# Token mixing, attention and FFN on one Trainium2 core: SyncE issues the loads of the next x behind the first sequence's probability exchange

## The reference

```
h = tok(x)                               # (64, 128, 192): per block of 16 rows q, k, v by small
                                         # matrices over the rows, softmax(q k'), q + attn v
h = h + attention(layernorm(h))          # 12 heads of 64, 3 kv heads, rope, softmax, Wo
h = h + ffn(layernorm(h))                # gelu(h @ W_in.T + b) @ W_out, 192 -> 768 -> 192
```

## Time and profile before

| | |
|---|---|
| median of 3 runs | 1170.94 us (1169.92 to 1171.51) |
| the profiled execution | 1165.9 us |
| its span, first to last instruction | 1163.6 us |
| PE busy | 995.3 us (86%) |
| DVE busy | 804.1 us (69%) |
| GpSimd (POOL) busy | 680.6 us (58%) |
| ACT busy | 664.2 us (57%) |
| SyncE's DMA queue | 121.05 MB, 37.9% of the 16 DMA engines' span |
| mean granted TensorE clock | 0.938 |

### The profile page before, as it was taken

How to read it: one execution, slowest core, us unless ns; L and a number is a source line. 1 busy time by engine, 2 the same in 40 slices (tenths; PEclk the granted TensorE clock), 3 DMA queues, 4 the chain that set the end, 5 groups by cost and what they waited for, 6 DMA issues and landing times.

```text
span 1163.6 us, 25886 instructions
## 1 busy us (share of the span) xinstructions
PE 995.3 (86%) x7402; PEld 836.9 (72%) x7402; DVE 804.1 (69%) x1996; ACT 664.2 (57%) x2501; POOL 680.6 (58%) x968
## 2 busy tenths in 40 slices
PE   7778988889888889888898888898888988888988
PEld 4667867768677677677686776776776867767777
DVE  4777766677667686666777676766767776767673
ACT  2555665646556556556565565655555655646564
POOL 2667565466655575655666555655556665556672
PEclk9999989899899899898999898998999998989999
DMA  5153334433344333344333443334443334433341
GB/s 169 28 136 108 92 104 133 124 99 88 88 133 133 98 102 87 112 133 119 98 93 88 133 133 97 100 85 117 133 119 108 85 88 133 133 97 94 102 116 48
DMA packets 193423, 124.68 MB, mean 107 GB/s; under 512 B 30720, under 2 KB 184960, under 8 KB 193408
## 3 DMA queue, kind: packets, MB, share of 16 engines
q1 hardware_dynamic: 190528, 121.05, 37.9%
q10 hardware_dynamic: 2880, 3.44, 0.9%
HBM read 69.39 MB, written 55.05 MB: 107 GB/s over the span
## 4 chain that ended last, share of the span: by engine, by line
PE 57%; DMA 16%; DVE 11%; SPq 9%; issue 5%; POOL 1%; ACT 1%; DVEq 0%; POOLq 0%
PE ring L1088 12%; PE ring L952 11%; PE ring L881 9%; DMA spill<-EB 8%; DMA ET<-spill 8%; PE bank L900 7%; PE ring L919 4%; DVE rot_s L597 4%; PE ring L859 3%; SPq L254 3%; SPq L236 3%; PE ring L1020 2%; PE bank L1055 2%; SPq L235 2%; PE ring L1047 2%
## 5 line engine op out<-in xcount | busy, mean ns | idle before, releaser
L330 ACT ACTIVATE E<-ring,m_neg 128x128 f32<-128x128 f32 x768 | 271.6, 373 | 17.0 <-DVE m_neg L603 16.0
L488 POOL TENSOR_TENSOR E<-E,e_rcp 128x512 f32<-128x512 f32 x158 | 176.6, 1126 | 40.4 <-DVE e_rcp L626 37.6
L480 POOL TENSOR_TENSOR qkT<-rot_c,rot_s 128x256 f32<-128x256 f32 x256 | 187.8, 734 | 20.1
L952 PE MATMUL ring<-ET,v_tok 128*64 128x512 f32 (+1 forms) x256 | 83.6, 799 | 111.9 <-DMA ET<-spill 111.5
L330 ACT ACTIVATION_READ_ACCUMULATOR E<-ring,m_neg 128x1 f32 x768 | 161.5, 210 | 0.0
L478 POOL TENSOR_TENSOR rot_s<-rot_s,rope_qs 128x256 f32<-128x256 f32 x192 | 145.9, 760 | 9.6 <-DVE rot_s L597 9.6
L1088 PE MATMUL ring<-wo_sb,OT 128*128 128x192 f32 x744 | 147.3, 352 | 0.0
L603 DVE TENSOR_REDUCE m_neg<-ring 128x4 f32<-128x512 f32 x192 | 129.9, 678 | 21.0 <-PE ring L919 21.0
L465 POOL TENSOR_SCALAR ve<-mv 128x1 f32<-128x1 f32 x64 | 14.0, 219 | 222.5 <-DVE mv L574 219.3
L900 PE MATMUL bank<-wout_sb,G 128*128 128x192 f32 x744 | 144.0, 330 | 0.0
L1088 PEld LDWEIGHTS ring<-wo_sb,OT 128*128 128x128 f32 x744 | 135.4, 211 | 8.7 <-issue 8.7
(11 more groups left out here) (156 smaller groups left out, 2646.3 us busy)
## 6 DMA issues: line engine op xcount, KB each, us to landing
spill<-EB SPq DMA_DIRECT2D x186, 256.0 KB, 2.7
ET<-spill SPq DMA_DIRECT2D x248, 128.0 KB, 2.8
ET<-spill SPq DMA_DIRECT2D x248, 64.0 KB, 2.4
x_sb<-in_x_dram SPq DMA_DIRECT2D x64, 192.0 KB, 2.5
out_dram<-out_sb SPq DMA_DIRECT2D x31, 192.0 KB, 2.1
x_sb<-in_x_dram SPq DMA_DIRECT2D x64, 64.0 KB, 2.3
w_raw<-in_w_att_dram ACTq DMA_DIRECT2D x2, 608.0 KB, 4.9
win_raw<-in_w_in_dram ACTq DMA_DIRECT2D x2, 384.0 KB, 6.1
```

The source lines that it names most:

```text
L330: last = nc.scalar.activation(E[:, a, s * P:(s + 1) * P], RING[a][:, s * P:(s + 1) * P], ACT.Exp, bias=m_neg[:, a, s:s + 1], accum_out=e_s ...
L480: nc.gpsimd.tensor_tensor(qkT[:, b, :, a], rot_c[:, b, :, a], rot_s[:, b, :, a], ALU.add).then_inc(q_out, 1)
L488: nc.gpsimd.tensor_tensor(e, e, r, ALU.mult).then_inc(prob_out, 1)
L952: last = nc.tensor.matmul(ring[k * HD:(k + 1) * HD, 512 * b:512 * b + n_cols], v[:, g * HD:(g + 1) * HD], src.rearrange("p i h c -> p i (h ...
```

## The change

In SyncE's step, the call that waits for h_mm and issues the four loads is moved from ahead of the exchange of sequence 0 to behind it. It stays ahead of the store.

```diff
             def step(p, att, ffn, fin, more):
                 if ffn and not (isinstance(p, int) and p == NP):
                     blocks_moved(1, p - 1)
-                if more:
-                    load_ahead(p + 2)
                 if isinstance(p, int) and p == 0:
...
                 elif att:
                     blocks_moved(0, p)
+                if more:
+                    load_ahead(p + 2)
                 if fin:
                     store(p - 2)
```

## The result

The changed kernel takes 1014.01 us (median of 3 runs, 1012.66 to 1015.53) against 1170.94 before. The ratio is 0.866, with a 95% interval of 0.864 to 0.868. The forecast was 1015 in a range of 1004 to 1043. The profiled execution is the one of 1014.01 us, with a span of 1011.7.

What follows compares the result with a forecast made beforehand. SyncE's queue was taken as the bound, x's loads and their wait for L1047 delaying the probability exchange. 1165.9 - 151.8 - 2.1 = 1012.0 us, taken as 1015 for the median's excess; range 1004 to 1043.

Steps and rivals of the forecast that it cites:

- Item 1: Exchange of sequence 0: spills move ahead of the loads and their wait for L1047, so L952 comes 3.71 us earlier.
- Item 2: PE behind L952: the clock stays up, so the slow stretch goes, 1.08 us in step 15.
- Items 3 and 4: Rest of the step unchanged, new step 30.20 us; 28 steps from 35.62 to 30.20 us save 151.8 us.
- Item 5: Step 1: the whole idle before L952 goes, 2.1 us; steps 0, 30 and 31 gain nothing.
- Items 6 and 7: Behind the moved loads: sequence 1's first spill slips some 0.1 us, x keeps 2.3 us margin or more; no cost.
- The rule on issue time: SyncE's loads: starting a DMA is usually small beside the DMA, so only the L1047 wait is won, some 1.2 us a step.
- A: Exchange before L952: the two DMA trips now bind, 1.0 us a step, 28 us more, 1043; chance 0.12.
- B: DVE and GpSimd bind: the late attention addition (L662) passes 0.3 us to every step, 8 us more, 1023; chance 0.10.
- C: L1016: x comes late and PE waits there, 28 us more than before, 1199; chance 0.02 in its slow form.
- D: Exchange: the change does nothing, something hidden from the profile held it; 1171, chance 0.03.

Runs made afterwards that it cites:

- the wait alone: Changed kernel with SyncE's wait for h_mm put back ahead of the exchange of sequence 0, the four loads staying behind it: 1044.5 us.
- spare loads: Changed kernel plus four DMAs of x's sizes into unread tiles, ahead of sequence 0's exchange in steps 2 to 29, without the h_mm wait: 1013.83 us.
- DVE turning first: Changed kernel with DVE turning sequence 0's first two groups (L617) before adding sequence 1's attention output (L662) and taking its statistics: 1013.39 us.
- x later still: Changed kernel with the four loads one exchange later, behind the spills and fills of sequence 1 in the next step: 1325.63 us.
- L900 moved: Changed kernel with two of sequence 0's six L900 matmul groups moved ahead of the token-mixing scores (L859): 1009.22 us, in the repeat 1013.78.

## Why the prediction was right, point by point

*The bound.* SyncE's queue ahead of the exchange was the bound, as read. The run with the wait alone and the one with spare loads take its two parts from each other: a late wait costs by itself, an issue only behind it.

*Item 1, the earlier start.* Forecast 3.71 us; L952 is 3.53 us closer to L1047 (11.26 to 7.73). The run with the wait put back prices the part for L1047 at 1.08; "the rest" of the 3.5 us in the forecast was 1.2.

*Item 2, the clock.* 1.08 in step 15 and the surplus of the mean over that step, 0.65, were 1.73 together. PE kept busy in the old order measured 1.79. The forecast took it without proof that the mean step is longer than step 15 because the slow stretch varies. The trace bears it out: steps 14 and 15 before took 36.35 and 34.97 us, and these are the windows of 4.4 us from the start of their L952, with the clock at 0.50 and 0.61.

```profile
543.56:547.96 4.40, 4.40 (x15) 2.36 (x16) 0.00 (x0) 1.45 (x3) 0.18 (x1) 0.50 0.62 176
579.72:584.12 4.40, 4.40 (x18) 2.66 (x19) 0.39 (x2) 1.82 (x4) 0.37 (x1) 0.61 0.64 179
```

The sum of 5.42 us a step came out as 35.62 - 30.14 = 5.48.

*Items 3 and 4.* L1088's end to the next L1047 is 18.11 us (509.57 to 527.68), forecast 18.05; 28 steps of 30.14 against 30.20 are 1.7 us less than forecast.

*Item 5.* Step 1 was to lose its 2.1 us of idle. From L1047 to the end of L1088 it takes 14.65 us (73.13 to 87.78) where it took 16.84: 2.19.

*The remainder.* The forecast for the profiled execution was 1012.0 and it took 1014.0. The steps gave 1.7 us more than forecast, but L1047 of step 1 starts at 73.13 instead of 69.56 us, 3.6 us later, in a part that the change leaves alone. It is not lost at once: the very first L1047 starts at 18.44 us, at 18.65 before. Windows of the steps behind it, before and after (the order of columns as above):

```profile
18.40:41.00 22.60, 15.59 (x116) 12.33 (x117) 15.58 (x40) 8.19 (x31) 16.55 (x21) 1.00 0.10 25
41.00:70.00 29.00, 24.80 (x190) 19.85 (x192) 21.72 (x56) 17.73 (x80) 19.43 (x27) 0.94 0.29 73
...
18.40:41.00 22.60, 17.93 (x116) 13.88 (x116) 13.84 (x35) 7.47 (x28) 14.82 (x20) 0.86 0.10 24
41.00:70.00 29.00, 24.10 (x170) 19.74 (x170) 19.66 (x52) 14.99 (x67) 18.17 (x26) 0.82 0.27 73
```

The clock of the first steps was lower in this execution. In the profile of the changed kernel's rerun step 2 begins at 107.2 us, here at 105.8, with DVE turning first at 102.9: this part varies by itself. The forecast also added 3 us for the excess of the median over the profiled execution, chosen by hand between 0 and 4.4; after the change the profiled execution is the median, so the excess was 0. That 1015 was hit to 1 us thus has luck in it: 3 us too many there and 1.7 in the steps, against 3.6 too few at the start. The steps are the firm part.

*Items 6 and 7.* The first spill of sequence 1 goes out at 508.09, 0.99 us behind the start of the store. That is 10.51 us behind L1047, where step 30 before had 10.14: a slip of 0.37 us, forecast 0.1. The fills behind it start 13.85 us behind L1047 (13.77), and no wait grew from it. x had 5.2 us from its last issue to L1016, against landings of at most 3.3. The margin was 1.9 us at the least, not the 2.3 or more of the forecast, and still enough.

*The rule on issue time*, which the prediction takes from the Trainium skill ("DMA: Bandwidth & Descriptors", section "Issuing engines are not separate DMA queues"), would have given about 1137. The trace had disagreed, and the result does too. The spare loads cost nothing, but not because an issue is short (0.40 and 0.47 us in the lines above): they stood away from the path.

*The rivals.* A did not come, but one thing in it was weak: I wrote that the clock would stay up behind about 1 us of wait, true at 1.19 us, and argued it by step 1's 2.14. One idle of that length is no proof: at 2.52 us the clock fell, and even at 2.12 and 2.16 (last section). B did not come in the sum. DVE's chain, which the one late addition in the earlier trace rows had hinted at, is close, and holds back the kernels in which DVE turns first. C needed x to land over 10 us after its issue, which it never came near; the run with x later still shows its mechanism, and a slow stretch dearer than I had allowed for that run. D fell with the result.

## What to carry to other kernels

On an in-order DMA queue look at what each wait holds up behind it: a wait that ends late, with transfers that nobody needs soon, belongs behind the urgent ones, and the issue of DMAs is free where the queue would idle anyway. If a kernel's last turns of a loop leave a part out, its trace already holds the experiment; the step without loads gave the new step to 0.1 us. And price an idle of TensorE with the slow stretch behind it: here it was a third of the whole gain.

## What was not expected of the hardware

The clock fell (0.65 in the 4.4 us behind) after an idle of 2.52 us, with full speed before it, while behind the 2.14 us of the earlier trace rows it stayed at 1.00. But the length of the idle ahead of L952 does not decide it alone. In the run with the wait alone, step 2 idled 2.16 us and the clock fell; in the run with half of the loads ahead, one step idled 2.47 us and it stayed up. PE and the windows behind, of these two runs:

```profile
113.98 2.83 PE L954 MATMUL ring<-ET,v_tok 128*64 128x512 f32 x8 [2.16 <-DMA ET<-spill]
113.98:118.40 4.42, 4.42 (x18) 2.38 (x19) 1.28 (x4) 1.71 (x4) 1.88 (x2) 0.64 0.79 206
...
287.00 1.69 PE L955 MATMUL ring<-ET,v_tok 128*64 128x512 f32 x8 [2.47 <-DMA ET<-spill]
287.00:291.42 4.42, 4.42 (x28) 3.20 (x29) 2.29 (x6) 3.05 (x6) 1.57 (x2) 1.00 0.85 234
```

In these two runs and the kernel before, the clock stayed at 1.00 behind each idle ahead of L952 of up to 1.77 us and fell behind each of 2.49 us or more; in between both were seen (the repeat with L900 moved fell behind 2.12 us). What decides there is open.

And the slow stretch is not of one length: in the kernel before, whose idle ahead of L952 was 3.66 to 4.08 us from step 3 on, the steps were between 34.7 and 36.5 us, and with PE kept busy between 33.6 and 34.1.
